# The last three expert tiles of the second batch: from gathered rows to products with matrices of shares

## The reference, cut to what matters

```python
cap = int(LOAD * K * max(1, T / E))          # K = 2, T = 512, E = 16: 64 slots for each expert
g = jnp.einsum('btc,ce->bte', x, w_router)
gate_probs = jax.nn.softmax(g, axis=-1)
top_k_probs, positions, indices, expert_inputs = jax.vmap(lambda xb, pb: _dispatch(xb, pb, cap))(x, gate_probs)
...
gg = jnp.einsum('enc,ech->enh', expert_inputs, w_gate)
h = jnp.einsum('enc,ech->enh', expert_inputs, w_fc)
h = jax.nn.silu(gg) * h
o = jnp.einsum('enh,ehc->enc', h, w_proj)
...
out = eo_b[ei_b, pos_b]                      # _collect: the rows of a token's two experts
return jnp.sum(tk_b[..., None] * out, axis=1)
```

## Time and profile before

| what | us |
|---|---|
| median of 3 runs without a profile | 1930.38 |
| lowest, highest of them | 1928.66, 1931.12 |
| profiled execution, its own time | 1917.37 |
| its span, which the rows' times are counted in | 1915.6 |
| TensorE busy | 1841.6 |
| VectorE busy | 1706.8 |
| ScalarE busy | 1457.6 |
| GpSimd busy | 45.9 |

### The profile page before, as it was taken

One profiled execution on the slowest core, in us unless ns is written; L12 is line 12 of the kernel. 1 busy time (PEld: TensorE's weight loads), 2 busy tenths in 40 slices (PEclk: granted clock), 3 DMA queues, 4 the chain that ended last, 5 costly groups with the idle time before them and its releaser, 6 DMA issues.

```text
span 1915.6 us, 56880 instructions
## 1 busy us (share of the span) xinstructions
PE 1841.6 (96%) x24652; PEld 812.1 (42%) x24652; DVE 1706.8 (89%) x1530; ACT 1457.6 (76%) x1660; POOL 45.9 (2%) x57
## 2 busy tenths in 40 slices
PE   8999999999999998999999999999998989998895
PEld 4444444444444443334444444444442445556431
DVE  6899999999999999979999999999998588788655
ACT  2699999999988987869998888989987465555121
POOL 2000000000000000000000000000000000001103
PEclk9999999999999999999999999999999999999998
DMA  8333333333333333322333333333333000005795
GB/s 262 119 95 100 105 98 101 106 106 106 101 95 98 99 84 101 111 68 78 90 101 84 84 90 90 96 90 96 89 79 122 24 1 1 2 1 207 245 307 165
DMA packets 113773, 196.21 MB, mean 102 GB/s; under 512 B 10352, under 2 KB 64624, under 8 KB 113520
## 3 DMA queue, kind: packets, MB, share of 16 engines
q1 hardware_dynamic: 110528, 183.33, 32.6%
q0 software_dynamic: 2560, 8.39, 1.3%
q10 hardware_dynamic: 432, 0.79, 0.1%
HBM read 109.63 MB, written 50.33 MB: 84 GB/s over the span
## 4 chain that ended last, share of the span: by engine, by line
PE 40%; DVE 40%; issue 15%; ACT 3%; DMA 1%; POOL 1%; DVEq 0%; POOLq 0%; SPq 0%; ACTq 0%
DVE dacc L1881 31%; PE ps L1217 8%; PE ps L1464 7%; PE ps L1116 4%; PE ps L1113 4%; PE ps L1306 3%; PE ps L1244 2%; DVE wsm L1824 2%; DVE wsm L2203 2%; PE ps L1346 2%; PE ps L1201 2%; PE ps L1269 2%; PE ps L1153 1%; PE ps L1301 1%; PE ps L1315 1%
## 5 line engine op out<-in xcount | busy, mean ns | idle before, releaser
L1733 ACT ACTIVATE pt<-ps,bias 128x1024 f32<-128x1024 f32 x1024 | 1096.9, 1114 | 182.0 <-PE ps L1464 99.2
L1881 DVE TENSOR_TENSOR dacc<-dacc,pt 128x2048 f32<-128x2048 f32 x496 | 1135.0, 2288 | 42.9 <-ACT pt L1733 16.2
L1464 PE MATMUL ps<-qst,kst 128*32 128x512 f16 x8192 | 620.7, 380 | 12.1 <-ACT pt L1733 10.1
L1217 PE MATMUL ps<-pt,vt 128*32 128x512 f32 x4096 | 485.1, 592 | 0.0
L1464 PEld LDWEIGHTS ps<-qst,kst 128*32 128x32 f16 x8192 | 211.6, 97 | 367.1 <-issue 153.4
L1116 PE MATMUL ps<-wsm 128*32 128x512 f16 x4608 | 314.9, 380 | 0.0
L1113 PE MATMUL ps<-wsm 128*32 128x512 f16 x4464 | 305.7, 379 | 0.0
L1217 PEld LDWEIGHTS ps<-pt,vt 128*32 128x32 f32 x4096 | 123.9, 110 | 211.0 <-issue 145.7
L1116 PEld LDWEIGHTS ps<-wsm 128*32 128x32 f16 x4608 | 125.4, 97 | 125.7 <-issue 3.2
L1113 PEld LDWEIGHTS ps<-wsm 128*32 128x32 f16 x4464 | 120.8, 97 | 121.0 <-issue 2.0
L1824 DVE SCALAR_TENSOR_TENSOR wsm<-ps,wsm 128x512 f16<-128x512 f32 x126 | 86.0, 683 | 8.1 <-ACT wsm L1549 8.0
(11 more groups left out here) (229 smaller groups left out, 1231.2 us busy)
## 6 DMA issues: line engine op xcount, KB each, us to landing
kst<-kscr SPq DMA_DIRECT2D x132, 256.0 KB, 3.5
kscr<-wsm SPq DMA_DIRECT2D x126, 256.0 KB, 3.5
kst<-kst SPq DMA_DIRECT2D x124, 256.0 KB, 3.4
wsm<-in_ctx SPq DMA_DIRECT2D x31, 768.0 KB, 5.3
wx<-in_gate SPq DMA_DIRECT2D x10, 512.0 KB, 8.2
wx<-in_fc SPq DMA_DIRECT2D x10, 512.0 KB, 9.5
wx<-in_proj SPq DMA_DIRECT2D x10, 512.0 KB, 9.2
qst<-qscr SPq DMA_DIRECT2D x32, 128.0 KB, 3.2
```

The costliest lines, as they stand in the source:

```text
L1217: p = e.matmul(ps[32 * h:32 * h + 32, 4 + n % 2, :], vt[:, kb % 2, ch, c:c + 32], pt[:, (2 * i + h // 2) % 6, h % 2, :], start=ch == 0, st ...
L1464: p = e.matmul(ps[r:r + 32, 2 * half + h2, :], kst[:, kb % 2, h, ch * 128 + r:ch * 128 + r + 32], qst[:, h, :], start=True, stop=True)
L1733: e.activation(pt[:, (2 * i + half) % 6], ps[:, 2 * half:2 * half + 2, :], ACT.Exp, bias=bias[:, 4 * kb + ch:4 * kb + ch + 1], scale=SCORE ...
L1881: e.tensor_tensor(own_heads, own_heads, probs, ALU.add).then_inc(S["add"], 1)
```

## The change

Batch 1's tiles 13, 14 and 15 (experts 10 to 15) are no longer stored and gathered. `STORED` is 13, `KEPT` 3, and `FIRST_KEPT` 640, the first slot row of the kept tiles; `obuf` of batch 1 has 640 rows.

- `picked(t)` on VectorE makes, for the 128 tokens of token tile 4 + t, a matrix of 128 x 384: the token's share where the column is the slot of one of its two choices, 0 elsewhere. It compares the slot numbers with `slots`, a row of 640 to 1023 that GpSimd writes with one `iota` after its scatters. The four stand after `hidden(3)` to `hidden(6)`.
- `e_mix(j)` on TensorE transposes the columns of kept tile j of these four matrices into bank 5, after the down projections of tiles 6, 7 and 8, and ScalarE copies them to `mix`.
- `e_share` multiplies `mix` with `oe`, so that a bank of PSUM gets for each token tile of batch 1 the sum over the kept tiles: four products for tile 13 ahead of tile 15's down projection, eight for tiles 14 and 15 behind it. The banks are 5, 0, 1 and 6, and `dn` counts them on.
- `near` makes gather indices `giu` for batch 1, at most 639, and shares `tg` that are 0 where a slot is kept. All 16 gathers stay; those of batch 1 wait for the stores of tiles 0 to 12.
- VectorE's end: the eight additions for batch 0 as before, then for each token tile of batch 1 an addition of its bank (L2348 of the changed kernel) and the two gathered ones.

```diff
 LAST_OF_FIRST = TILES.index((0, 7))
+STORED = 13
+KEPT = 16 - STORED
+FIRST_KEPT = 128 * TILES[STORED][1]
+SHARED_BANKS = (5, 0, 1, 6)
 FOLLOWS = {TILES.index((1, p)): p + 4 for p in range(4)}
...
  score nmx prob scale pT tcD tcA cut value aT wom x3 lvar lroot lstat xn3 rT rC rM lg
+ one cT cC
  lgs pexp ohb cum cumr dst ciu sctA sctB eT xeT up sgx hN hP hT dn oe os0 os1 y out
...
         xbuf = [nc.dram_tensor(f"xbuf{b}", [3072, 512], F32).ap() for b in range(2)]
-        obuf = [nc.dram_tensor(f"obuf{b}", [1024, 512], F32).ap() for b in range(2)]
+        obuf = [nc.dram_tensor(f"obuf{b}", [(1024, FIRST_KEPT)[b], 512], F32).ap() for b in range(2)]
         fx = {"q": nc.dram_tensor("fq", [2, 512, 512], F32).ap(),
...
         diuE = sb("diuE", [128, 3], U32)
+        giu = sb("giu", [128, 2, 4], U32)
+        gf = sb("gf", [128, 2, 4], F32)
+        tg = sb("tg", [128, 2, 4], F32)
         s3 = ExitStack()
...
         og = sb("og", [128, 16, 512], F32, s6)
+        pick = xn3[:, 4:4 + KEPT, :].rearrange("p a n -> p (a n)").rearrange("p (t n) -> p t n", n=128 * KEPT)
+        other, slots = xn3[:, 7, 0:128 * KEPT], og[:, 15, 0:128 * KEPT]
+        mix = xn3[:, 0:KEPT, :]
         s6.close()
...
                 x = i - 2
-                if x < 0:
+                if x < 0 or x >= STORED:
                     continue
...
+        slotted = 0
+
         def pool(e):
+            nonlocal slotted
             d = Count()
...
                 e.indirect_dma_start(out=og[:, 8 * k + t, :], out_offset=None, in_=obuf[t // 4],
-                                     in_offset=bass.IndirectOffsetOnAxis(ap=ciu[:, k, t:t + 1], axis=0)
+                                     in_offset=bass.IndirectOffsetOnAxis(
+                                         ap=ciu[:, k, t:t + 1] if t < 4 else giu[:, k, t - 4:t - 3], axis=0)
                                      ).then_inc(G[t], 16)
...
                 scatter(diu[:, k, t:t + 1], t)
+            e.wait_ge(S["sctB"], 128)
+            e.iota(slots, pattern=[[1, 128 * KEPT]], base=FIRST_KEPT, channel_multiplier=0,
+                   allow_small_or_imprecise_dtypes=True).then_inc(S["pool"], 1)
+            slotted = d.up()
             e.wait_ge(S["ciu"], 2)
...
                 if t % 4 == 0:
-                    stored = LAST_OF_FIRST + 1 if t == 0 else 16
+                    stored = LAST_OF_FIRST + 1 if t == 0 else STORED
+                    if t:
+                        e.wait_ge(S["ciu"], 3)
                     e.wait_ge(S["os0"], 16 * ((stored + 1) // 2))
...
                 p.then_inc(S["dn"], 1)
+
+            def e_mix(j):
+                e.wait_ge(S["one"], 4)
+                if j:
+                    e.wait_ge(S["cC"], j)
+                for t in range(4):
+                    p = e.transpose(ps[:, 5, t * 128:t * 128 + 128], pick[:, t, 128 * j:128 * j + 128], ident[:])
+                p.then_inc(S["cT"], 1)
+
+            def e_share(t, tiles):
+                for x in tiles:
+                    if t == 0:
+                        e.wait_ge(S["oe"], x + 1)
+                    p = e.matmul(ps[:, SHARED_BANKS[t], :], mix[:, x - STORED, t * 128:t * 128 + 128], oe[:, x % 2, :],
+                                 start=x == STORED, stop=x == 15)
+                if tiles[-1] == 15:
+                    p.then_inc(S["dn"], 1)
...
                     e_down(x - 2)
+                if 8 <= x < 8 + KEPT:
+                    e_mix(x - 8)
             e_down(14)
             e_back(15)
+            e.wait_ge(S["cC"], KEPT)
+            e.wait_ge(S["xeT"], 16)
+            e.wait_ge(S["hN"], 15)
+            for t in range(4):
+                e_share(t, (13,))
             e_down(15)
+            for t in range(4):
+                e_share(t, (14, 15))
...
                 if x > 1:
-                    e.wait_ge(S[f"os{s}"], 16 * (x // 2))
+                    e.wait_ge(S[f"os{s}"], 16 * min(x // 2, (STORED + 1 - s) // 2))
                 e.activation(oe[:, s, :], ps[:, 3 + s, :], ACT.Copy).then_inc(S["oe"], 1)
...
+            def e_mix(j):
+                e.wait_ge(S["cT"], j + 1)
+                e.activation(mix[:, j, :], ps[:, 5, :], ACT.Copy).then_inc(S["cC"], 1)
+
             e_up(0)
...
                     e_down(x - 2)
+                if 8 <= x < 8 + KEPT:
+                    e_mix(x - 8)
             e_down(14)
...
+            def near():
+                rows, part_ = ci[:, :, 4:8], tp[:, :, 4:8]
+                e.wait_ge(S["ciu"], 2)
+                e.tensor_scalar(gf[:], rows, FIRST_KEPT - 1.0, None, ALU.min).then_inc(S["dve"], 1)
+                e.wait_ge(S["dve"], own.up())
+                e.tensor_copy(giu[:], gf[:]).then_inc(S["ciu"], 1)
+                e.scalar_tensor_tensor(out=tg[:], in0=rows, scalar=FIRST_KEPT - 1.0, in1=part_, op0=ALU.is_le,
+                                       op1=ALU.mult).then_inc(S["dve"], 1)
+                own.up()
+
+            def picked(t):
+                e.wait_ge(S["pool"], slotted)
+                if t:
+                    e.wait_ge(S["one"], t)
+                e.tensor_scalar(pick[:, t], slots, ci[:, 0, 4 + t:5 + t], tp[:, 0, 4 + t:5 + t], ALU.is_equal,
+                                ALU.mult).then_inc(S["dve"], 1)
+                e.tensor_scalar(other, slots, ci[:, 1, 4 + t:5 + t], tp[:, 1, 4 + t:5 + t], ALU.is_equal,
+                                ALU.mult).then_inc(S["dve"], 1)
+                own.up()
+                e.wait_ge(S["dve"], own.up())
+                e.tensor_tensor(pick[:, t], pick[:, t], other, ALU.add).then_inc(S["one"], 1)
+
+            def gathered(t):
+                e.wait_ge(G[t], 32)
+                for k in range(2):
+                    share = tp[:, k, t:t + 1] if t < 4 else tg[:, k, t - 4:t - 3]
+                    done = S["y"] if k else S["dve"]
+                    e.scalar_tensor_tensor(out=xs[:, t, :], in0=og[:, 8 * k + t, :], scalar=share, in1=xs[:, t, :],
+                                           op0=ALU.mult, op1=ALU.add).then_inc(done, 1)
+                    if k == 0:
+                        e.wait_ge(S["dve"], own.up())
+
             for x in range(1, 16):
...
                 hidden(x)
+                if x == 2:
+                    near()
+                if 3 <= x < 7:
+                    picked(x - 3)
             turned_hidden(15)
-            for t in range(8):
-                e.wait_ge(G[t], 32)
-                e.scalar_tensor_tensor(out=xs[:, t, :], in0=og[:, t, :], scalar=tp[:, 0, t:t + 1], in1=xs[:, t, :],
-                                       op0=ALU.mult, op1=ALU.add).then_inc(S["dve"], 1)
+            for t in range(4):
+                gathered(t)
+            for t in range(4, 8):
+                e.wait_ge(S["dn"], 16 + t - 3)
+                e.tensor_tensor(xs[:, t, :], ps[:, SHARED_BANKS[t - 4], :], xs[:, t, :], ALU.add).then_inc(S["dve"], 1)
                 e.wait_ge(S["dve"], own.up())
-                e.scalar_tensor_tensor(out=xs[:, t, :], in0=og[:, 8 + t, :], scalar=tp[:, 1, t:t + 1], in1=xs[:, t, :],
-                                       op0=ALU.mult, op1=ALU.add).then_inc(S["y"], 1)
+                gathered(t)
```

## The result

| | median, us | lowest, highest | runs |
|---|---|---|---|
| before | 1930.28 | 1925.91, 1931.38 | 14 |
| after | 1933.32 | 1930.96, 1939.65 | 14 |

The ratio is 1.0023, with an interval of 1.0014 to 1.0032: slower by 0.23%, 3.0 us, and outside the predicted range. The profiled execution of after took 1932.27 us, its span is 1930.5.

What follows compares the result with a forecast made beforehand. GpSimd's gathers, with a 6.9 us pause, were taken to bound the tail; afterwards VectorE's chain, ending at 1908.8 including 1.5 for the loop, plus 2.4 gives span 1911.2 against 1915.6. So 1930.38 - 4.4 = 1926.0 us, range 1923.2 to 1930.0.

Steps and rivals of the forecast that it cites:

- the addition of the trace's difference to the median: Whole kernel: the 4.4 us gained in the traced span were taken off the unprofiled median, 1930.38, giving 1926.0.
- the term for VectorE's start: Tail: VectorE adds the first half from 1891.79, four pairs of 1.45 us, until 1897.6.
- the five cases: Rivals to the forecast: late gathers 0.19, clock 0.03, one row 0.02, not hidden 0.08, more gain 0.08.
- The wait that goes: GpSimd's tail: the pause before the ninth gather vanishes, sixteen gathers follow each other, a gain of 7.1 us there.
- The blocks of transposes: TensorE's tile loop: three blocks of four transposes, unhidden, at 0.5 us each delay everything behind by 1.5 us.
- VectorE's picks and the iota: Tile loop: four picks of about 1.4 us fit in VectorE's 2.78 us idle; the iota is counted as zero.
- TensorE's and VectorE's end: Tail: VectorE waits 0.9 us for the first bank, then 2.17 per tile, ending at 1908.8; span ends 2.4 later.
- Gathers against VectorE: Tail: the sixteenth gather lands at 1906.0, VectorE wants it at 1907.3, so 1.3 us in hand; VectorE bounds.
- case 1: Rival, tail: gathers issued beside VectorE's additions and landing among stores come late, +2.5 us, 1928.5; chance 0.19.
- case 2: Rival, tail: TensorE's clock falls to 1.2 GHz during the products of shares, up to 1936.5 us; chance 0.03.
- case 3: Rival, tail: 210 choices reading row 639 of `obuf1` slow the last eight gathers, 1934.7 us; chance 0.02.
- case 4: Rival, tile loop: a pick isn't hidden or the loop is held up elsewhere, 2 us more, 1928.0; chance 0.08.

Runs made afterwards that it cites:

- condition B: State of the machine in the other five of six follow-up sessions, where the kernel before took 1929.1 to 1930.4 us; the result's measurement belongs to it.
- e1_before: The kernel before, unchanged under a new name, run again in condition A: 1918.82 us, 0.9999 of before.
- condition A: State of the machine in the first of six follow-up sessions, where the kernel before took 1918.2 us; the trace of before is like those.
- e2_before: The kernel before, unchanged, run again for its profile in condition B: a single execution of 1926.61 us beside 1929.14.
- e1_after: The changed kernel, unchanged, run again in condition A: 1914.28 us, 0.9983 of before.
- e2_loop_only: The kernel before plus the loop's matrices, transposes, copies and iota, all 16 tiles stored and gathered, no products with shares; in condition B: 1931.68 us, 1.0008.
- e1_held: The changed kernel with GpSimd's ninth gather held until ScalarE has evicted tile 15, in condition A: 1921.46 us, 1.0020 of before.

## Why the prediction was wrong, by its own steps

**The step that failed** is the addition of the trace's difference to the median: 13 us between the profiled execution and the median "which I take as common to both kernels". They were not common; they were the mark of condition B, in which the trace of before had not been taken. With it failed the term for VectorE's start, read from that trace: "as soon as it is through with `hT`: 1891.79", which is 4.3 us after hT(14). In after VectorE starts its first addition 14.6 us after hT(14) (1913.32 against 1898.68), since the copy hT(15) stood still for 10.96 us, a wait that the sum has at nothing. e1_before's profiled execution took 1920.40 beside a median of 1918.82 without a profile, so a gap of 13 us was not the price of profiling. Of the five cases none had TensorE's counts late, and slower had a chance of 0.05 through other mechanisms. In condition A the forecast holds: -4.4 us was forecast, -3.9 measured, and the spans are 5.2 apart. That it is so near is luck in part. The loop cost 0.7 us more than forecast and the stretch behind hT(15) 0.85 more (19.10 against 18.25), while the kernel before had itself 0.75 more behind hT(15) in e1_before than in the trace that the forecast was read from (24.90 against 24.15).

**The wait that goes**: right in both conditions. In condition B it is also the cause of the loss. The pause after the eighth gather, 7.96 us in e2_before, was where hT(15) came through (the ninth gather, then the copy):

```profile
1906.94 0.94 POOL L1066 DMA_INDIRECT og<-obuf,ciu  x1 [7.96 <-issue]
```

```profile
1900.68 0.42 DVE L2249 COPY hT<-ps 128x256 f32<-128x256 f32 x1 [1.65 <-PE ps L1255]
```

Eight issues that ended at 1898.99 left it 1.0 us later than in condition A (4.98 against 3.95), sixteen leave it 11 us later. From hT(15) to the end after is 6.8 us shorter (17.4 against 24.2), the standstill costs 9.9 and the loop 2.2: +5.3, what the medians of that session show.

**The blocks of transposes**: right in kind, mis-sized. The chain of e1_after has, for one tile with a block and one without:

```profile
1861.34 0.59 PE ps L1299 x4
1861.93 3.58 PE ps L1265 x16
...
1868.18 3.43 PE ps L1265 x16
```

0.59 for the block and 0.15 more for the up projection that now follows it: 0.74 each, 2.2 us for three, where 1.5 was forecast. The 0.53 that was called an upper bound was none: the block alone took more, and a part of its cost shows in the products behind it. e2_loop_only, which has this work alone, took 2.5 us more than before (1.0008, 0.9998 to 1.0019), which agrees within its noise.

**VectorE's picks and the iota**: hidden, as counted. A pick leaves 1.41 us of the 2.78 that VectorE is idle per tile. The iota took 0.45 us. ScalarE's copies cost nothing.

**TensorE's and VectorE's end**: right in condition A. The wait for the first bank was 0.99 us (0.9 forecast), then 2.18 from tile to tile (2.17), and 2.4 us from the end of the last addition to the span's. The two rows behind the step of TensorE's products stand 0.42 us apart, not the 0.43 of the text; in e1_after eight of them took 3.53 us, 0.44 each.

**Gathers against VectorE** (case 1): the 1.3 us in hand were used up. Four of the eight issues beside VectorE's additions took 1.09 to 1.24 us instead of 0.95 (0.83 us in all, where case 1 had 2.8), the gathers by `giu` landed after a median of 5.1 us, and the last pair waited 0.71, for a gather that landed 6.0 us after its start, where 4.65 was counted and 5.7 was case 1's bound. That is the mechanism of case 1, in small. The Trainium skill ("SBUF — State Buffer", Who interferes with whom) has the rule for it, a VectorE instruction with two SBUF inputs against GpSimd's reads; the rows agree in part: the longer issues all stand beside such additions and in after, beside an idle VectorE, the gathers took 0.95 each, but two issues of e1_after beside additions (1895.31 and 1902.11) took 0.95 as well. The prediction's argument against case 1, the even 1.255 of the first eight, had no weight by that rule, since VectorE's work beside them reads at most one input from SBUF. The standstill is something else: from 1906 to 1910 VectorE did nothing that GpSimd could contend with.

**The clock** (case 2): it did fall, as a consequence. In after the granted clock is 1.00 up to 1910, with TensorE idle since 1906.04, then 0.61 over 1910 to 1913 and 0.50 over 1913 to 1917 (the level of 1.2 GHz), and the last down projection takes 3.68 us instead of 1.94. It hides behind VectorE's 5.88 us of additions: the first bank is whole at 1919.26, and VectorE starts on it at 1919.28. **One row** (case 3): no sign of it; the gathers by `giu` start 1.25 to 1.45 apart and land 0.9 us later than the others (5.1 against 4.2), but in e1_held, where the same gathers by `giu` run later and beside less work, they land as the others do (3.8 against 3.9). **Not hidden** (case 4): no.

## What to carry to other kernels

Before adding a difference read from a trace to a median, see whether the traced execution took the time that the runs take; a gap of 0.7% says that the trace shows another condition, and then the sign of a 0.2% forecast is not known. A pause of an engine can be what lets others through: ask what happens in it before closing it. A stream of indirect DMAs is best broken where another engine's last count is due; here, in condition B, one wait on that very count cost 2.7 us of GpSimd's time and saved 8.3.

## What the runs showed of the hardware that I had not expected

- In condition B a row of indirect DMAs, issued 0.30 us apart, holds up what TensorE reports to the other engines. VectorE's count came 0.8 to 3.0 us after the row's end, so it waited 4.6 us with ten in a row, 6.7 with twelve and 11 to 12.4 with sixteen; a count due earlier came through in the middle of a row, some 8 us late. Ten iotas in a row (5.16 us) do not. The counts of the DMAs' own landings were not held up, and VectorE's last one for TensorE was not either: in after its hidden rows are done at 1902.01 and TensorE transposes them from 1902.16. Nor are the first few issues enough: with five of them made, hT(14) came in time (an idle of 2.78 us ahead of it, as in before).
- The scatters ahead of the experts seem to do the same in the kernel before; no run takes them away. GpSimd and VectorE in e2_before, with the last of eight and the last of three scatters:

```profile
1757.03 0.96 POOL L1062 DMA_INDIRECT xbuf<-xn,diu  x1 [0.30 <-issue]
...
1789.74 0.96 POOL L1062 DMA_INDIRECT xbuf<-xn,diuE  x1 [0.30 <-issue]
```

```profile
1759.46 0.96 DVE L2054 RECIPROCAL pr<-ps 128x128 f32<-128x128 f32 x1 [3.18 <-remote]
...
1791.56 0.96 DVE L2054 RECIPROCAL pr<-ps 128x128 f32<-128x128 f32 x1 [4.62 <-remote]
```

  VectorE goes on 1.47 and 0.86 us after these issues end. In e1_before the first of the two does not wait, and the second waits 2.18 us. So before loses some 5.6 us here and 1.0 at hT(15). The spans of e1_before and e2_before are 6.3 apart; their medians are 10.9 apart, so a part of what condition B costs is not in these two traces (e1_before's traced execution took 1.6 us more than its median, e2_before's 2.5 less than its session's).
- While those eight scatters were issued, TensorE's 64x128 products had 0.36 to 0.58 us idle between them in e2_before; in e1_before twelve of them took 1.35 us together. Beside the gathers of after its products ran on at full pace and only the counts were late. Whether it is TensorE's queue, the way of the counts or something ahead of both is not settled by these runs, nor what makes a session condition A or B: the same chip showed both.
- What GpSimd's row shows is the issue, 0.95 us; the data landed a median of 3.8 to 5.4 us after it began, in the traces that show it. The Trainium skill ("Perfetto Trace Analysis", DMA Instruction — SWDGE) says the same of this kind of DMA, that its end in the profile is that of the making of descriptors and not of the data's way, and these rows agree.
